# Constant products in TensorE's planned idle gaps, and an order planned at one clock: four chained transformer layers on one core

## What is computed

```python
def _attn(q, k, v, causal):
    s = jnp.einsum('blhd,bmhd->bhlm', q, k)
...
    p = jax.nn.softmax(s, axis=-1)
    return jnp.einsum('bhlm,bmhd->blhd', p, v)
```

```python
            logits = h @ rw.T + rb
            vals, idx = jax.lax.top_k(logits, K)
            gates = jax.nn.softmax(vals, axis=-1)
...
            h1 = jax.nn.gelu(jnp.einsum('nd,efd->enf', hf, fc1_w) + fc1_b[:, None, :], approximate=False)
            eo = jnp.einsum('enf,edf->end', h1, fc2_w) + fc2_b[:, None, :]
```

```python
                h = h * dec[:, :, None, None] + u[..., None] * bt[:, None, None, :]
                y = jnp.einsum('bhpn,bn->bhp', h, ct)
```

## Time and profile before

| | |
|---|---|
| median of 3 runs | 3803.47 us (3802.98 to 3811.05) |
| profiled execution, device time | 3809.99 us |
| its span from first to last instruction | 3808.2 us |
| PE busy | 3637.7 us, 96% |
| DVE, ACT, POOL busy | 2643.2, 2795.5, 987.4 us |
| mean granted clock of PE | 0.99 |
| HBM read and written | 82.80 and 4.19 MB, 23 GB/s |

### The profile page before, as it was taken

How to read it: one execution, slowest core, us unless ns; L and a number is a source line. 1 busy time by engine, 2 the same in 40 slices (tenths; PEclk the granted TensorE clock), 3 DMA queues, 4 the chain that set the end, 5 groups by cost and what they waited for, 6 DMA issues and landing times.

```text
span 3808.2 us, 86916 instructions
## 1 busy us (share of the span) xinstructions
PE 3637.7 (96%) x32576; PEld 2538.4 (67%) x32576; DVE 2643.2 (69%) x5516; ACT 2795.5 (73%) x4922; POOL 987.4 (26%) x1348
## 2 busy tenths in 40 slices
PE   6989999999999999999999999999999999999987
PEld 3556767676766667666676666666666676667664
...
GB/s 66 2 3 25 28 43 33 24 24 34 2 43 14 24 34 24 21 14 32 25 24 23 21 24 25 24 34 23 21 14 32 25 24 21 14 27 25 35 14 7
DMA packets 52615, 92.56 MB, mean 24 GB/s; under 512 B 11816, under 2 KB 35312, under 8 KB 51952
## 3 DMA queue, kind: packets, MB, share of 16 engines
...
HBM read 82.80 MB, written 4.19 MB: 23 GB/s over the span
## 4 chain that ended last, share of the span: by engine, by line
PE 54%; DVE 9%; ACT 6%; issue 2%; POOL 2%; DMA 1%; SPq 0%; DVEq 0%; POOLq 0%; ACTq 0%
PE ps L1172 11%; PE ps L1249 8%; PE ps L1241 6%; PE ps L1184 6%; PE ps L1162 5%; PE ps L1192 3%; PE ps L1131 2%; DVE mx L1544 2%; PE ps L1157 2%; PE ps L1204 2%; DVE pr L1550 2%; PE ps L1140 1%; PE ps L1290 1%; ACT xh L1347 1%; PE ps L1115 1%
## 5 line engine op out<-in xcount | busy, mean ns | idle before, releaser
L1544 DVE TENSOR_REDUCE mx<-ps 128x8 f32<-128x616 f32 (+1 forms) x704 | 671.5, 954 | 347.0 <-PE ps L1162 330.3
L1397 ACT ACTIVATE pt<-ps 77x512 f32<-77x512 f32 (+1 forms) x1408 | 765.5, 593 | 159.7 <-PE ps L1172 156.4
L1735 POOL TENSOR_TENSOR kx<-kT,in_tiles 128x308 f32<-128x308 f32 (+1 forms) x384 | 316.0, 823 | 1008.2 <-PE ps L1162 942.2
L1172 PE MATMUL ps<-k_sb,pr 128*77 128x128 f32 (+1 forms) x3776 | 532.2, 280 | 13.0 <-ACT pr L1388 3.8
L1388 ACT ACTIVATE pr<-pr 128x616 f32<-128x616 f32 (+1 forms) x472 | 394.4, 841 | 152.8 <-DVE pr L1550 151.9
L1172 PEld LDWEIGHTS ps<-k_sb,pr 128*77 128x77 f32 (+1 forms) x3776 | 416.9, 146 | 118.3 <-issue 72.9
L1241 PE MATMUL ps<-hT,ew 128*128 128x512 f32 x1024 | 486.8, 602 | 4.5 <-DVE pr L1550 2.1
L1550 DVE TENSOR_TENSOR pr<-ps,mx 128x616 f32<-128x616 f32 (+1 forms) x472 | 450.3, 954 | 16.2
L1184 PE MATMUL ps<-pt,v 77*16 77x128 f32 (+2 forms) x11264 | 436.1, 276 | 13.6 <-ACT pt L1397 10.0
L1406 ACT ACTIVATE og<-ps 128x256 f32<-128x256 f32 x704 | 263.2, 379 | 196.5 <-PE ps L1184 194.1
L1184 PEld LDWEIGHTS ps<-pt,v 77*16 77x16 f32 (+2 forms) x11264 | 252.3, 97 | 195.8 <-issue 109.0
...
## 6 DMA issues: line engine op xcount, KB each, us to landing
ew<-weights SPq DMA_DIRECT2D x128, 512.0 KB, 4.6
...
```

Of the source, the lines that this page charges most:

```text
L1172: i = tr(p[0:keys, j * L:(j + 1) * L], probs[s][pl.slot(unit, 3)][:, c:c + keys], ident)
L1397: go_act(pt[s][0:keys, q % 2, :], p[0:keys, :], ACT.Copy).then_inc(probsT_ready.sem, 1)
L1544: link(v_.tensor_reduce(m, tile, AX.X, ALU.max, negate=True))
L1735: tell(pool, g_.tensor_tensor(spread_keys[s][:, pl.slot(step, 2), 0:4 * keys].rearrange("p (h k) -> p h k", h=4), kT[s][:, b * keys:(b + 1 ...
```

## The change

Three things. The planner no longer knows a half clock: a PE step costs its time at the full one. Where a PE step starts 1.0 us or more after PE came free in the plan (`GAP`), the plan notes it in `spare` with a bank that nobody uses at that moment and a count, 55% of the gap divided by 0.225 us; PE then issues that many bfloat16 products of the constants `ident16` and `causal16`, 512 columns each, into that bank ahead of the step. Nothing reads them. And the table `CHANGES` is another one, for stretches of 80 planned us. Besides, the plan gives up the experts' tile at the end of the last `down` on VectorE where it was its end on TensorE; what SyncE waits for on the chip is as before. All experts are computed before and after.

```diff
+GAP, FILL, SPARE_WORK = 1.0, 0.55, 0.225
...
-    half, window, active = [True], [0], [0.0]
-
-    def pass_windows(t):
...
-    def at_clock(t, length):
...
+    spare = {}
...
-        length = at_clock(t, chain[k][1]) if engine == P else chain[k][1]
-        end = t + length + (SWITCH if switch else 0.0)
+        if engine == P and t - free[P] >= GAP:
+            unused = [b for b in range(8) if bank_free[b] + HOP <= free[P]]
+            if unused:
+                spare[step] = min(unused, key=lambda b: bank_free[b]), int(FILL * (t - free[P]) / SPARE_WORK)
+        end = t + chain[k][1] + (SWITCH if switch else 0.0)
...
-            if final(stream_of(step)) == step and engine == P:
+            if final(stream_of(step)) == step and engine == chain[-1][0]:
                 held[which], freed[which] = None, end + HOP
...
-STRETCH = 60
+STRETCH = 80
 CHANGES = [
     {"LEAD": 0.928713073, "scores": {P: 1.4}, "z": {P: -4.2, A: -4.2}},
-    {"LEAD": 0.928713073, "STAY": 5.34060906, 5: -6.6, "scores": {P: 0.6}, "out": {P: -0.9, V: -0.9},
-     "pairs": {P: 4.6, V: 3.5}, "z": {P: -4.2, A: -4.2}},
+    {"LEAD": 0.928713073, 0: 1.3, "scores": {P: 0.3}, "bias_mlp": {G: 4.9}, "z": {P: -4.2, A: -4.2},
+     "gate_norm": {G: 1.3}, "final": {A: 0.9}},
...
         for step in self.order[P]:
+            if step in self.spare:
+                self.spare_before[step] = last.get(self.spare[step][0])
...
-                for old in pl.before[step]:
+                if step in pl.spare:
+
+                    b, count = pl.spare[step]
+                    old = pl.spare_before[step]
+                    if old:
+                        released = RELEASED[old[0]]
+                        pe.wait_ge(released.sem, pl.ordinal[released.engine, old])
+                    for _ in range(count):
+                        mm(ps[:, b, :].rearrange("p (h k) -> p h k", h=4), ident16,
+                           causal16.unsqueeze(1).broadcast_to([128, 4, 128]), start=True, stop=True)
+                for old in pl.before.get(step, ()):
```

More of the change, by code:

```diff
@@ new lines @@
+    {"gates": {P: 0.2, V: 0.4, A: 4.6}, "store": {G: 1, Y: 1.4}},
+    {"bias": {G: -4.7}, "scores": {P: 0.1}, "gates": {P: 0.2, V: 0.4, A: 4.6}, "store": {G: 1, Y: 1.4}},
+    {"STAY": 2.90978142, "bias": {G: -4.7}, "scores": {P: 0.1}, "gates": {P: 0.2, V: 0.4, A: 4.6},
+     "store": {G: 1, Y: 1.4}},
+    {"STAY": 2.90978142, "bias": {G: -4.7}, "scores": {P: 0.1}, "out": {V: 2.7}, "gates": {P: 0.2, V: 0.4, A: 4.6},
+     "decay": {A: 3.1}, "store": {G: 0, Y: 1.4}},
+    {"LEAD": 4.88827486, "STAY": 2.90978142, "bias": {G: -8.4}, "scores": {P: 0.1}, "out": {V: 2.7},
+     "gates": {P: 0.2, V: 0.4, A: 4.6}, "decay": {A: 3.1}, "store": {G: 0, Y: 1.4}},
@@ new lines @@
+    {"LEAD": 4.88827486, "STAY": 2.90978142, "bias": {G: -8.4}, "scores": {P: 0.1}, "out": {V: 2.7},
+     "gates": {P: 0.2, V: 0.4, A: 4.6}, "decay": {A: 3.1}, "store": {G: 0, Y: 1.4}},
+    {"LEAD": 4.88827486, "STAY": 2.90978142, "bias": {G: -8.4}, "scores": {P: 0.1}, "out": {V: 2.7},
+     "gates": {P: 0.2, V: 0.4, A: 4.6}, "decay": {A: 3.1}, "store": {G: 0, Y: 1.4}},
+    {"LEAD": 4.88827486, "STAY": 2.90978142, "bias": {G: -13.2}, "scores": {P: 0.1}, "out": {V: 2.7},
+     "gates": {P: 0.2, V: 0.4, A: 4.6}, "decay": {A: 3.1}, "store": {G: 0, Y: 1.4}},
@@ new lines @@
+    {"LEAD": 4.51941968, "STAY": 2.58184902, "bias": {G: -13.2}, "scores": {P: 0.1}, "out": {V: 2.7},
+     "gates": {P: 0.2, V: 0.4, A: 4.6}, "step_size2": {V: -1.4}, "decay": {A: -0.6}, "gate_norm": {G: 2.1},
+     "store": {G: 0, Y: 1.4}},
+    {"LEAD": 4.51941968, "STAY": 2.58184902, "bias": {G: -13.2}, "scores": {P: 0.1}, "out": {V: 2.7},
+     "gates": {P: 0.2, V: 0.4, A: 4.6}, "up": {A: 0.8}, "step_size": {A: -2.9}, "step_size2": {V: -1.4},
+     "decay": {A: -0.6}, "gate_norm": {G: 2.1}, "store": {G: 0, Y: 1.4}},
@@ new lines @@
+    {"LEAD": 4.51941968, "STAY": 1.12213573, "bias": {G: -13.2}, "scores": {P: 0.1}, "out": {V: 2.7},
+     "hidden": {A: 2.1}, "fetch": {Y: 4.1}, "gates": {P: 0.2, V: 0.4, A: 4.6}, "up": {A: 0.8},
+     "step_size": {A: -0.8}, "step_size2": {V: -0.5}, "decay": {A: -0.6}, "gate_norm": {G: 2.1},
+     "mamba_out": {P: 3.5, V: 4.6}, "store": {G: 0, Y: 1.4}},
+    {"LEAD": 4.51941968, "STAY": 1.12213573, "bias": {G: -13.2}, "scores": {P: 0.1}, "out": {V: 2.7},
+     "hidden": {A: 2.1}, "fetch": {Y: 4.1}, "route": {P: 0.4, V: 3.7, A: 1.3}, "gates": {P: 0.2, V: 0.4, A: 4.6},
+     "up": {A: 0.8}, "step_size": {A: -0.8}, "step_size2": {V: -0.5}, "decay": {A: -0.6}, "gate_norm": {G: 2.1},
+     "mamba_out": {P: 3.5, V: 4.6}, "store": {G: 0, Y: 1.4}},
@@ new lines @@
+    {"LEAD": 4.51941968, "STAY": 1.12213573, "bias": {G: -13.2}, "scores": {P: 0.1}, "out": {V: 2.7},
+     "hidden": {A: 2.1}, "project": {A: 0.7}, "fetch": {Y: 4.1}, "route": {P: 0.4, V: 3.7, A: 1.3},
+     "gates": {P: 0.2, V: 0.4, A: 4.6}, "up": {A: 0.8}, "step_size": {A: -0.8}, "step_size2": {V: -0.5},
+     "decay": {A: -0.6}, "gate_stats": {V: 1, G: 1.8}, "gate_norm": {G: 3.1}, "mamba_out": {P: 3.5, V: 4.6},
+     "store": {G: 0, Y: 1.4}},
+    {"LEAD": 3.77021974, "STAY": 1.12213573, "bias": {G: -13.2}, "scores": {P: 0.1}, "out": {V: 2.7},
+     "hidden": {A: 2.1}, "project": {A: 0.7}, "fetch": {Y: 4.1}, "route": {P: 0.4, V: 3.7, A: 1.3},
+     "gates": {P: 0.2, V: 1.4, A: 4.6}, "up": {A: 0.8}, "step_size": {A: -0.8}, "step_size2": {V: -0.5},
+     "decay_in": {G: 15.6}, "decay": {A: -0.6}, "gate_stats": {V: 1, G: 1.8}, "gate_norm": {G: 3.1},
+     "mamba_out": {P: 3.8, V: 4.6}, "store": {G: 0, Y: 1.4}},
@@ L727, in __init__ @@
     def __init__(self, streams):
-        self.begins, self.banks, self.holders = timetable(streams)
+        self.begins, self.banks, self.holders, self.spare = timetable(streams)
         self.place = {step: (n, m) for n, steps in enumerate(streams) for m, step in enumerate(steps)}
@@ L738, in __init__ @@
                 self.ordinal[engine, step] = count[step[0]]
-        self.before, last = {}, {}
+        self.before, self.spare_before, last = {}, {}, {}
         for step in self.order[P]:
+            if step in self.spare:
+                self.spare_before[step] = last.get(self.spare[step][0])
             if step in self.banks:
```

198 lines of the change are left out of this document (59 added, 139 removed).

## The result

The changed kernel takes 3835.12 us in the median of 4 runs (3828.26 to 3837.62), the kernel before beside it 3805.32 us (3802.98 to 3811.05): a ratio of 1.0073, 95% interval 1.0055 to 1.0091. It is slower, and 9 us beyond the upper end of the predicted range. The profiled execution spans 3832.5 us, 24.3 more than the 3808.2 of before.

The account below looks back on a forecast made before the run. The prediction took the amount of PE work to bound the middle, with order mattering at start, end and short waits. Terms +1 + 7 + 3 - 5 = +6 us on 3803.5 gave 3810 us, range 3790 to 3826.

Parts of the forecast that it names:

- The middle: Dense stretch of expert passes: between -4 and +12 us, taken as +3, with PE 97.5 to 98% busy.
- Most repeats unchanged ... Two small waits can be counted: Step on the middle: expert fetches cost nothing new; PE's waits change by +3 us for `route` and -4 for `out`.
- The third: Passes 7 and 10: first `turn` stands closer behind its `scores`; nine such `turn` steps fall short by 11.5 us together.
- Both warnings: Signs that the forecast is wrong: the middle loses a microsecond or more per pass, or the last pieces shrink.
- starved start and short distances: Rival, slower, chance 0.24: PE waits where less work separates `scores` from `turn`; start costs 9.8, distances 11.5, 3826 us.
- The start: Before the first expert product: 47.1 us of work moves there from the middle, costing +3.0 to +9.8 us, taken as +7.
- The end: Last passes: more work beside the last pass's chain, gain between 0 and -17.8 us, taken as -5.
- best end: From `norm` 7 of pass 14, pieces keeping their lengths: 247.4 us against 265.2 before on equal terms, -17.8 us.
- The four pieces: The last pass's chain: 27, 34, 30 and 52 us before; near 27-30, 34-37, 30-33 and 52-58 us after.
- The products: 81 constant products, 20.7 us, nearly all in time PE would wait: cost +1 us, gain 0 in the sum.
- Products in the way: Rival, slower, chance 0.04: gaps are not where planned, 20.7 us of products land on the path, 3824 us and more.
- clock and end: Rival, faster, chance 0.16: products and third stream hold full clock in the last 120 us; 3779 us at best, 3790.

Follow-up runs that it names:

- e3: Changed kernel with `gates` behind the fourth `hidden` and one `up` ahead of `expert_bias` in passes 6 to 13: 3823.62 us, 1.0038 to the kernel before.
- e4: Changed kernel with GpSimd's decays (sequences 2 and 3, passes 5 to 12) and MLP bias (passes 7 to 14) cut to one column: 3820.02 us, 1.0032.
- e9: e4 with GpSimd's `weigh` products of pass 0 also cut to one column of each head: 3816.24 us, 1.0028 to the kernel before.
- e12: Changed kernel with `load` and `stats` 0 moved behind `pairs` and `conv` 0 on VectorE in passes 5 and 6: 3838.59 us, 1.0076.
- e1: Changed kernel's order without its 81 constant products: 3835.46 us, 1.0076 to the kernel before.
- e2: Kernel before, own order, plus 97 constant products in 31 places by the 1.0 us rule: 3802.17 us, 0.9987.
- e7: Kernel before, own order, plus 197 constant products in 112 idle places of 0.42 us or more: 3791.99 us, 0.9963.
- e6: Changed kernel with 188 products in 121 places of 0.42 us or more, in place of 81 in 27: 3835.86 us, 1.0074.
- e10: Kernel before with the 0.42 us rule's products only from 3400 us of the plan on, 79 in 34 places: 3793.18 us, 0.9969.

## Why the prediction was wrong

**The middle: +3 predicted, +34 measured**, or +32 up to `norm` 7 of pass 14, where the prediction's end begins. This is the term that failed: 96.9% busy where 97.5 to 98% were named. The step "Most repeats unchanged ... Two small waits can be counted" took the places where PE's order had a new neighbour and stopped at three. The two counted ones were right: `route` +2.6 for +3, `out` -4.3 for -4. The third, the first `turn` behind `scores`, I let reach up to 11.5; PE's waits for `turn` (L1172, L1146) grew from 2.1 to some 4 us. What was missing is `gates`. The orders show that it moved ahead of two `hidden` in eight passes. In passes 7 to 12 GpSimd's decays and bias now fall into the same microseconds as VectorE's logits; in passes 6 and 13 they did so before, where the later place of `gates` hid it. I read PE's order only, though the trace of before had operations of 1.1 to 1.4 us among those of 0.43. e3 and e4 take this out from either side: 12 and 15 us. By the table e4 lowers the middle from 34.4 to 17.1. The eight waits are 11 of these 17 us; part of the rest may be clock, since that one execution has one stretch of 3.4 us at half clock between 400 and 3400 us where the changed kernel has five. Of the 17 us left, e9 shows the same contention once more, without a gain, and e12 a load that arrives late for passes 5 and 6. The rest stands in the table of waits: `mix` +5.0, `down` +3.9, `norm` +2.9, `up` +2.4 and `turn` +2.1 us. No run took them apart, and their cause stays open; some 10 us of the loss that e4 leaves fall between 400 and 1000 us of work.

Both warnings in the prediction came true: the middle lost more than a microsecond per pass, namely two, and three of the last four pieces shrank. The rival "starved start and short distances" was right in its sign and in its place, PE waiting in a middle that its new order left with shorter distances. Its mechanism (`scores` to `turn`) was a small part: `turn` and the `mix` behind it wait 7.1 us more, 11.5 was its price, and the larger loss is `gates`.

**The start: +7 predicted, +6.7 measured.** The first expert product comes at 426.03 us, predicted about 425, and PE is busy 91% until then, a little more than the 80 to 90% named. The hit is partly luck. In e1 the same order has 10.0 us at this point. And the sum priced idle time alone, while the changed kernel also has two stretches of 3.4 us at half clock in its start (at 133 and 181 us) where the one before has one; no run takes the two apart.

**The end: -5 predicted, -17 measured from 3400 us of work on.** By the prediction's own marks, from `norm` 7 of pass 14, it is 250.6 us against the 265.2 on equal terms: -14.6, between the -5 taken and the best end of -17.8. The four pieces, predicted at 27 to 30, 34 to 37, 30 to 33 and 52 to 58 us, took 24.9, 30.4, 28.9 and 55.1. The premise that pieces keep their lengths, because they were long on VectorE and ScalarE, was wrong in part: e2 and e7 show that the half clock made the second and third longer. In the new order these pieces run at the full clock without a product as well (e1). Pass 13's `out` comes 88 us before the end, some 100 predicted. The three terms that follow the loss, 6.7 + 34.4 - 16.8, sum to the 24.3 us.

**The products: +1 and no gain predicted, 0 measured**, within some 7 us (e1 against the changed kernel, e6). "Products in the way" is dead. But the reason why they bring nothing here is not that the clock had nothing to give: with the order of before they bring 5 us at the 1.0 us rule and 14 us at the 0.42 us rule. The rival "clock and end" had the right mechanism for the end. The stretches at half clock from 3500 us on add up to 59 us before, 9 in e7, 20 in the changed kernel and 33 in e1, the new order without products. So the order alone takes away nearly half of that time; that the products then had too little left to win fits these numbers, but no run tests it by itself. The Trainium skill's advice on gaps, page "TensorE: Matmul & The Clock Gate", section "Why this matters for your kernels", which I had weighed against the trace, holds for the end of the old order (e7, e10), where the stretches at half clock shrink and the time falls. At 1757 us the stretch stays in e7, as expected.
